# The recurrence of a macaron layer as 86 chunks of 24 tokens in place of 228 chunks of 9

## The reference, cut to what matters

```python
B_all = einsum('bsd,nd->bsn', xn, B_w) + B_b
states = A_pow * cumsum(B_all / max(A_pow, 1e-8))          # a linear scan over the tokens
ssm_out = einsum('bsn,dn->bsd', states, C_w) + C_b
def step(h, xt):                                           # 4096 tokens, one after the other
    cat = concatenate([xt, h])                             # 1024 + 512
    ff1 = tanh(cat @ ff1_w.T + ff1_b)
    ff2 = tanh(cat @ ff2_w.T + ff2_b)
    t_i = sigmoid((cat @ ta_w.T + ta_b) * 0.1 + (cat @ tb_w.T + tb_b))
    return ff1 * (1 - t_i) + t_i * ff2
out = x + h_all @ out_w.T + out_b
```

## Time and profile before

| | us |
|---|---|
| median of 3 runs | 1722.78 |
| lowest and highest of them | 1721.22, 1829.82 |
| the profiled execution | 1719.35 |
| its span on the slowest core | 1717.8 |
| spans of the 8 cores | 1714.5 to 1717.8 |
| first matmul of the recurrence | 874.89 |
| first matmul of the projection behind it | 1084.68 |

### The profile page before, as it was taken

One profiled execution on the slowest core, in us unless ns is written; L12 is line 12 of the kernel. 1 busy time (PEld: TensorE's weight loads), 2 busy tenths in 40 slices (PEclk: granted clock), 3 DMA queues, 4 the chain that ended last, 5 costly groups with the idle time before them and its releaser, 6 DMA issues. The chain is left out here.

```text
span 1717.8 us, 29950 instructions; the slowest of 8 cores (1714.5 to 1717.8 us)
## 1 busy us (share of the span) xinstructions
PE 1279.5 (74%) x9089; PEld 860.0 (50%) x9107; DVE 1172.6 (68%) x2126; ACT 958.1 (56%) x1428; POOL 642.6 (37%) x668
## 2 busy tenths in 40 slices
PE   0000087698898998998659987357699999998999
PEld 0000065465565665654348866135465655655644
DVE  4898568687687776774266666458776776777741
ACT  0426167766776766674246654146666666665651
POOL 0000322555756746547500024221633535334332
PEclk9999999899999999999869999579999999998999
DMA  9590210212122221114120000111111111200111
GB/s 290 176 334 4 62 38 13 62 37 51 38 50 62 62 51 38 51 38 118 55 50 2 2 1 2 52 59 50 50 50 64 61 50 56 81 26 26 50 38 62
DMA packets 35765, 105.66 MB, mean 62 GB/s; under 512 B 4756, under 2 KB 14100, under 8 KB 34584
## 3 DMA queue, kind: packets, MB, share of 16 engines
q1 hardware_dynamic: 24568, 95.08, 16.7%
q0 software_dynamic: 11040, 8.66, 3.5%
HBM read 84.58 MB, written 25.70 MB: 64 GB/s over the span
## 5 line engine op out<-in xcount | busy, mean ns | idle before, releaser
L587 PE MATMUL bank<-xqT,w1q 128*128 128x258 bf16 (+1 forms) x4352 | 575.4, 277 | 111.2 <-DVE y L891 110.6
L587 PEld LDWEIGHTS bank<-xqT,w1q 128*128 128x128 fp8e4 x4352 | 417.4, 100 | 277.4 <-issue 149.3
L608 PE MATMUL bank<-w2q,q 128*128 128x512 fp8e4 x2112 | 535.2, 383 | 0.0
L921 DVE SCALAR_TENSOR_TENSOR y<-bank,convws,y 128x256 f32<-128x256 f32 (+1 forms) x544 | 256.4, 471 | 270.3 <-ACT y L738 269.2
L1055 POOL TENSOR_TENSOR y<-y,Rb 128x1024 f32<-128x1024 f32 (+1 forms) x136 | 322.8, 2403 | 179.3 <-ACT Rb L763 179.3
L738 ACT ACTIVATE y<-bank,convbs,convws 128x256 f32<-128x256 f32 (+1 forms) x544 | 293.1, 551 | 165.0 <-PE bank L587 161.3
L608 PEld LDWEIGHTS bank<-w2q,q 128*128 128x128 f16 x2112 | 206.1, 98 | 166.1 <-issue 7.9
L891 DVE SCALAR_TENSOR_TENSOR y<-bank,convws,y 128x256 f32<-128x256 f32 (+1 forms) x544 | 253.8, 467 | 0.1
L689 ACT ACTIVATE y<-y 128x1024 f32<-128x1024 f32 (+1 forms) x136 | 139.9, 1029 | 149.5 <-DVE y L891 149.3
L832 DVE TENSOR_TENSOR M<-M,ab 128x1024 f32<-128x1024 f32 (+1 forms) x119 | 199.4, 1676 | 2.2 <-ACT ab L701 2.2
L711 ACT ACTIVATE q<-y,qoff 128x1024 f16<-128x1024 f32 (+1 forms) x136 | 151.8, 1117 | 65.8 <-POOL y L1055 62.3
(11 more groups left out here) (159 smaller groups left out, 1328.7 us busy)
## 6 DMA issues: line engine op xcount, KB each, us to landing
raw<-w1T SPq DMA_DIRECT2D x8, 2048.0 KB, 35.2
raw<-w2T SPq DMA_DIRECT2D x8, 2048.0 KB, 17.8
xg<-xall SPq DMA_DIRECT2D x18, 512.0 KB, 5.2
x1t<-xall SPq DMA_DIRECT2D x17, 512.0 KB, 4.1
basebuf<-x1t SPq DMA_DIRECT2D x17, 512.0 KB, 3.1
xg<-basebuf SPq DMA_DIRECT2D x16, 512.0 KB, 4.6
x2buf<-xg SPq DMA_DIRECT2D x16, 512.0 KB, 2.9
x1t<-x2buf SPq DMA_DIRECT2D x16, 512.0 KB, 4.3
```

The source lines that it names most:

```text
L587: mm = pe.matmul(pA[n % 4][:, 0:tw + 2], w1q[:, c, k * P:(k + 1) * P], xqT[j % 3][:, c, 0:tw + 2], start=c == 0, stop=c == DC - 1)
L608: pe.matmul(pB[e % 2][:], q[:, qs, kh, :], w2q[:, kh, 512 * h:512 * h + 512], start=kh == 0, stop=False)
L921: dve.scalar_tensor_tensor(v, pA[n % 4][:, 0:tw], convws[:, 3 * k:3 * k + 1], v, ALU.mult, ALU.add).then_inc(conv1_done, 1)
```

## The change

The chunks become longer and fewer: 86 chunks of 24 tokens, so 17 + 24 = 41 steps of 86 columns. The gate blocks of a step are no longer taken one by one. They lie in four banks of PSUM, and consecutive steps use the two halves of the eight banks in turn. For each half of the hidden units one bank holds ff1 and ff2 (four blocks, 344 columns) and one holds the time gate (two blocks, 172 columns). ScalarE takes a bank with one tanh, so 4 in a step, and VectorE makes half of the hidden units with one `mixd`, `mixu`, `hcur` of 172 columns, so 6 in a step.

A bias column can't serve a bank with several blocks, so the biases are added by TensorE: one matmul for each block with the transposed biases `bT` (44 rows: the values in bf16 in rows 0 to 11, what the rounding left in rows 32 to 43) and `pick`, which is 1 in the rows of that block. That makes 72 matmuls of 86 columns in a step: 12 for biases, 12 of `Wp`, 48 of `Wh`. `b44`, `pick` and `bT` are made ahead of the recurrence, on VectorE with one transpose on TensorE. The four `Wh` parts are taken in two groups, parts 0 and 1 when the first half of `hcur` is there, parts 2 and 3 when the second is. And `bias_dve` is moved from behind the last step to between steps 0 and 1.

```diff
-CN = 228
-CL = 9
+CN = 86
+CL = 24
 CW = 17
-SJC = 230
+SJC = CN + 1
...
-    gate = [[at(f'gate{i}{j}', GB + (3 * j + i) * 928, [P, CN]) for j in range(2)] for i in range(3)]
-    mixd = [at(f'mixd{j}', GB + 5568 + j * 928, [P, CN]) for j in range(2)]
-    mixu = [at(f'mixu{j}', GB + 5568 + 1856 + j * 928, [P, CN]) for j in range(2)]
-    assert GB + 5568 + 3712 <= YB + YR * T * 4
-    hcur = [at(f'hcur{j}', MB + j * 1824, [P, KC, CN], BF16) for j in range(2)]
+    st_ = at('states', YB + 16384 + 8704, [P, WLEN + 16])
+    sJ = at('sJ', YB + 16384 + 8704 + 8768, [P, CL, SJC], BF16)
+    GB = YB + 16384 + 8704 + 8768 + 4192
+    gateF = [at(f'gateF{i}', GB + i * 1376, [P, 2, 2, CN]) for i in range(2)]
+    gateT = [at(f'gateT{i}', GB + 2752 + i * 704, [P, 2, CN]) for i in range(2)]
+    mixd = [at(f'mixd{i}', GB + 4160 + i * 704, [P, 2, CN]) for i in range(2)]
+    mixu = [at(f'mixu{i}', GB + 5568 + i * 704, [P, 2, CN]) for i in range(2)]
+    pick = at('pick', GB + 6976, [P, 12, CN], BF16)
+    b44 = at('b44', GB + 9056, [P, 44])
+    bT = at('bT', GB + 9248, [P, P], BF16)
...
+    def ssm_pe():
+        pe.wait_ge(bias_in, 4)
+        pe.wait_ge(bsb_done, 17)
+        pe.transpose(pM[0:44, 0:P], b44[:], idf[:]).then_inc(bias_mm, 1)
...
+        dve.wait_ge(round_done, 8 * NT1)
+        dve.scalar_tensor_tensor(bcr[:, 8:12], bcr[:, 8:12], 0.1, bcr[:, 12:16], ALU.mult, ALU.add).then_inc(bias_in, 1)
+        dve.memset(b44[:], 0.0).then_inc(bias_in, 1)
+        dve.wait_ge(bias_in, 2)
+        dve.tensor_copy(b44[:, 0:12], bcr[:, 0:12]).then_inc(bias_in, 1)
+        dve.tensor_copy(b44[:, 32:44], bcr[:, 0:12]).then_inc(bias_in, 1)
+        dve.tensor_tensor(pick[0:44], idb[0:44, 0:12].unsqueeze(2).to_broadcast([44, 12, CN]),
+                          idb[0:44, 32:44].unsqueeze(2).to_broadcast([44, 12, CN]), ALU.add)
...
-        dve.scalar_tensor_tensor(bcr[:, 8:12], bcr[:, 8:12], 0.1, bcr[:, 12:16], ALU.mult, ALU.add).then_inc(ssm, 1)
-        dve.wait_ge(ssm, 7)
-        dve.tensor_scalar(bcr[:, 8:12], bcr[:, 8:12], 0.5, None, ALU.mult)
+        dve.wait_ge(ssm, 6)
         dve.tensor_copy(carry[:], st_[:, 2047:2048])
         dve.tensor_scalar(tofs[:], tofs[:], 2048.0, None, ALU.add)
-        dve.tensor_copy(sJ[:], st_[:, 108:108 + CL * SJC].rearrange('p (c k) -> p k c', k=CL))
+        dve.tensor_copy(sJ[:], st_[:, 126 - CL:126 - CL + CL * SJC].rearrange('p (c k) -> p k c', k=CL))
+        dve.wait_ge(bias_mm, 1)
+        dve.tensor_copy(bT[0:44, :], pM[0:44, 0:P]).then_inc(ssm, 1)
+        dve.wait_ge(ssm, 7)
+        dve.tensor_tensor(bT[32:44, :], pM[32:44, 0:P], bT[32:44, :], ALU.subtract)
...
-            pool.wait_ge(h_done, 4 * s + 4)
+            pool.wait_ge(h_done, 2 * s + 2)
             pool.tensor_copy(hv[:, :, :, s - CW], hcur[s % 2][:]).then_inc(hc_done, 1)
...
+    def slots(half, kind):
+        if kind == 0:
+            return [(2 * f + c, 512 * f + P * (2 * half + c), 4 * f + 2 * half + c) for f in range(2) for c in range(2)]
+        return [(c, 1024 + P * (2 * half + c), 8 + 2 * half + c) for c in range(2)]
     def cfc_pe():
+        parts = [(half, kind) for half in range(2) for kind in range(2)]
         for s in range(NSTEP):
             u = s - CW
-            s_in = sJ[:, u % CL, u // CL + 2:u // CL + 2 + CN]
+            s_in = sJ[:, u % CL, u // CL + 1:u // CL + 1 + CN]
             h_in = hcur[(s + 1) % 2]
-            def cols(i):
-                c0 = 512 * (i % 3) + P * (i // 3)
-                return slice(c0, c0 + P)
-            for i in range(6):
-                n = 12 * s + i
-                if n >= 8:
-                    pe.wait_ge(gate_done, n - 7)
-                mm = pe.matmul(bank[n % 8][:, 0:CN], Wp[:, cols(i)], s_in, start=True, stop=s == 0)
+            gb = bank[4 * (s % 2):4 * (s % 2) + 4]
+            for i, (half, kind) in enumerate(parts):
+                if s >= 2:
+                    pe.wait_ge(gate_done, 4 * (s - 2) + i + 1)
+                for at_, c0, r in slots(half, kind):
+                    o = gb[i][:, CN * at_:CN * at_ + CN]
+                    pe.matmul(o, bT[0:44, :], pick[0:44, r, :], start=at_ == 0, stop=False, skip_group_check=True)
+                    mm = pe.matmul(o, Wp[:, c0:c0 + P], s_in, start=False, stop=s == 0, skip_group_check=True)
                 if s == 0:
                     mm.then_inc(gate_mm, 1)
             if s:
-                for kk in range(KC):
-                    pe.wait_ge(h_done, 4 * (s - 1) + kk + 1)
-                    for i in range(6):
-                        n = 12 * s + i
-                        mm = pe.matmul(bank[n % 8][:, 0:CN], Wh[:, kk, cols(i)], h_in[:, kk, :], start=False, stop=kk == KC - 1)
-                        if kk == KC - 1:
-                            mm.then_inc(gate_mm, 1)
-            for i in range(6, 12):
-                n = 12 * s + i
-                if n >= 8:
-                    pe.wait_ge(gate_done, n - 7)
-                mm = pe.matmul(bank[n % 8][:, 0:CN], Wp[:, cols(i)], s_in, start=True, stop=s == 0)
-                if s:
-                    for kk in range(KC):
-                        mm = pe.matmul(bank[n % 8][:, 0:CN], Wh[:, kk, cols(i)], h_in[:, kk, :], start=False, stop=kk == KC - 1)
-                mm.then_inc(gate_mm, 1)
+                pe.wait_ge(h_done, 2 * (s - 1) + 1)
+                for i, (half, kind) in enumerate(parts):
+                    for at_, c0, r in slots(half, kind):
+                        o = gb[i][:, CN * at_:CN * at_ + CN]
+                        for kk in range(2):
+                            pe.matmul(o, Wh[:, kk, c0:c0 + P], h_in[:, kk, :], start=False, stop=False, skip_group_check=True)
+                pe.wait_ge(h_done, 2 * (s - 1) + 2)
+                for i, (half, kind) in enumerate(parts):
+                    for at_, c0, r in slots(half, kind):
+                        o = gb[i][:, CN * at_:CN * at_ + CN]
+                        for kk in range(2, 4):
+                            mm = pe.matmul(o, Wh[:, kk, c0:c0 + P], h_in[:, kk, :], start=False, stop=kk == 3, skip_group_check=True)
+                    mm.then_inc(gate_mm, 1)
     def cfc_act():
         for s in range(NSTEP):
-            for i in range(12):
-                n = 12 * s + i
-                b, f = i // 3, i % 3
-                act.wait_ge(gate_mm, n + 1)
-                if n >= 6:
-                    act.wait_ge(h_done, (n - 6) // 3 + 1)
-                act.activation(gate[f][b % 2][:], bank[n % 8][:, 0:CN], AF.Tanh, bias=bcr[:, 4 * f + b:4 * f + b + 1],
-                               scale=0.5 if f == 2 else 1.0).then_inc(gate_done, 1)
+            gb = bank[4 * (s % 2):4 * (s % 2) + 4]
+            for half in range(2):
+                if s:
+                    act.wait_ge(h_done, 2 * (s - 1) + half + 1)
+                act.wait_ge(gate_mm, 4 * s + 2 * half + 1)
+                act.activation(gateF[half][:].rearrange('p f b c -> p (f b c)'), gb[2 * half][:, 0:4 * CN], AF.Tanh).then_inc(gate_done, 1)
+                act.wait_ge(gate_mm, 4 * s + 2 * half + 2)
+                act.activation(gateT[half][:].rearrange('p b c -> p (b c)'), gb[2 * half + 1][:, 0:2 * CN], AF.Tanh,
+                               scale=0.5).then_inc(gate_done, 1)
     def cfc_dve():
         for s in range(NSTEP):
-            for b in range(4):
-                n = 4 * s + b
-                f1, f2, tt = gate[0][b % 2], gate[1][b % 2], gate[2][b % 2]
-                hh = hcur[s % 2][:, b, :]
-                dve.wait_ge(gate_done, 3 * n + 2)
-                dve.tensor_tensor(mixd[b % 2][:], f2[:], f1[:], ALU.subtract).then_inc(mix_d, 1)
-                dve.wait_ge(gate_done, 3 * n + 3)
+            if s == 1:
+                bias_dve()
+            for half in range(2):
+                n = 2 * s + half
+                f1, f2, tt = gateF[half][:, 0], gateF[half][:, 1], gateT[half][:]
+                hh = hcur[s % 2][:, 2 * half:2 * half + 2, :]
+                dve.wait_ge(gate_done, 4 * s + 2 * half + 1)
+                dve.tensor_tensor(mixd[half][:], f2, f1, ALU.subtract).then_inc(mix_d, 1)
+                dve.wait_ge(gate_done, 4 * s + 2 * half + 2)
                 dve.wait_ge(mix_d, n + 1)
-                dve.scalar_tensor_tensor(mixu[b % 2][:], tt[:], 1.0, mixd[b % 2][:], ALU.add, ALU.mult).then_inc(mix_u, 1)
+                dve.scalar_tensor_tensor(mixu[half][:], tt, 1.0, mixd[half][:], ALU.add, ALU.mult).then_inc(mix_u, 1)
                 dve.wait_ge(mix_u, n + 1)
                 if s >= CW + 2:
                     dve.wait_ge(hc_done, s - CW - 1)
-                if s in (CW - CL, CW):
-                    c = 1 if s == CW - CL else 0
-                    dve.scalar_tensor_tensor(hh, mixu[b % 2][:], 0.5, f1[:], ALU.mult, ALU.add).then_inc(mix_h, 1)
-                    dve.wait_ge(mix_h, b + 1 + (4 if s == CW else 0))
-                    dve.tensor_tensor(hh[:, c:c + 1], hh[:, c:c + 1], pcs[:, 4:5], ALU.mult).then_inc(h_done, 1)
```

(31 more changed lines are left out.)

## The result

The changed kernel takes 1793.2 us (median of 5 runs) against 1721.2 for the kernel before: a ratio of 1.042, with a 95% interval of 1.041 to 1.043. It is slower by 4.2%, where I had forecast 1689 and a range of 1679 to 1715. The profiled execution has a span of 1791.6 us on its slowest core (core 2).

What follows compares the result with a forecast made beforehand. TensorE's 60 matmuls and their chain bound warm-up steps; GpSimd's copy adds 2.2 us to late ones. Recurrence 26.9 plus projection 5.8 saves 32.7 us: 1686.7 profiled, 1690.1 median, 1689 taken; range 1679 to 1715.

Steps and rivals of the forecast that it cites:

- A step after the change, TensorE's share: Recurrence step: 72 matmuls of 86 columns at 0.038 us each, 2.7 us, where 60 matmuls took 6.31.
- The sign that was named: Recurrence: a matmul spacing above 0.047 us would make the forecast wrong upward, as would a late `mixd` over 0.5.
- half clock: Recurrence: TensorE, working 2.7 of 3.8 us, stays at half clock; 5.5 us a step, 1751 us; chance 0.04.
- The rival that ended slower: Recurrence: short matmul pairs have a TensorE floor of 0.078 us or more; at 0.095, 1803 us; chance 0.08.
- The chain: Recurrence step: 0.75 us from `hcur` to first tanh, then 3.01 through VectorE's six operations; 3.76 us a step.
- ScalarE's slope: Tanhs in the recurrence: ScalarE costs 0.84 ns a column, so 0.55 us for 344 columns and 0.41 for 172.
- The last 24 steps: End of the recurrence: 4.0 us a step, with GpSimd copying 344 columns in place of 912.
- The copy's block on `mixd`: Last 24 steps: GpSimd's copy blocks VectorE until 1.44 us after `hcur`, `mixd` wants 1.41; 0.1 a step counted.
- the rival of a block until the copy's end: Last 24 steps: the copy holds `mixd` until it ends, 0.5 us a step, 12 more, 1701 us; chance 0.10.
- The projection: Behind the last `hcur`: copy and release to first matmul take some 2.4 us in place of 8.16, 5.8 less.
- The wait for `obr`: Step 1: VectorE waits for the moved bias row's DMA, landing up to 12.7 us after issue; some 10 us lost.
- The start: Ahead of the recurrence: making `pick` and `bT` delays GpSimd by 1.0 us and adds 0.6, together 1.6 us.

Runs made afterwards that it cites:

- with 128 rows: Changed kernel with the bias matmuls padded with zeros from 44 to all 128 rows, nothing else edited; 1676.5 us, 0.975 of before.
- without bias matmuls: Changed kernel with the bias matmuls left out of the loop, so the gates have no biases; 1677.1 us, 0.975 of before.
- both kernels with 24 changes a step: The changed kernel (44-row bias matmuls), 1793.2 us, and its padded version with 64 rows in the bias matmuls, 1792.1 us.
- the chunks alone: Kernel before with only the new sizes, 86 chunks of 24 tokens, and nothing else of the change; 1719.5 us, 0.999 of before.

## Why the prediction was wrong

**The step that failed is "A step after the change, TensorE's share".** It gave all 72 matmuls of a step a spacing of 0.038, taken from runs of matmuls of one shape, and said of the 44-row ones only that no row shows them. The bounds, 0.025 and 0.095, came from matmuls and weight loads with 128 rows too, so they could not hold what lay outside: 0.143 for each of the 24 alternating matmuls. The bias matmuls were then costed at nothing by the slack of 0.2 us that this spacing left. The runs put 24 x 0.104 = 2.5 us a step on the alternation. No rival was made of a change of row count between neighbours. The sign that was named, a spacing above 0.047, did come.

**The clock.** The rival "half clock" came true in part, and its reason did not: it made the clock depend on TensorE's idle share. In the changed kernel the records show no idle time and the clock is 0.71; with 128 rows TensorE is idle for 5.8 of 40 us, without bias matmuls for 10.9, and the clock is 1.00. What is shown is that the clock fell in both kernels with 24 changes a step (0.71 and 0.74) and was at 0.99 or more from 905 to 1035 in every variant of the changed kernel with 8 or fewer. But the alternation is not needed for it: the chunks alone, where all matmuls have 128 rows, have 0.88 from 905 to 1075, with falls to 0.50 (from 1002 to 1004, for one), and TensorE is recorded busy there for 79% of the time, less than with 128 rows in the changed kernel and more than without bias matmuls. Why the clock falls is open, also because the records can't show what TensorE does between the starts. Its price, 48 `Wh` matmuls 0.072 apart and not 0.039, is 1.6 us a step. Together with the 2.5 that makes 4.1, of which the slack of about a microsecond takes part; measured are 3.0 (6.80 against 3.79). That the clock alone would be worth 1.6 is worked out, not shown by a run of its own.

**The rival that ended slower** set a floor for every short pair, with 0.078 as the point of decision. The mean over the step is indeed 6.80 / 72 = 0.094, so its side and its price were right (0.095 gave 1803). That was luck: 0.095 was the recorded length of a weight load, and 0.094 is a mean of 24 matmuls 0.143 apart and 48 that are 0.072 apart. Its mechanism was wrong, since the same pairs with 128 rows come 0.039 apart. The Trainium skill's rule (TensorE: Matmul & The Clock Gate, "Back-to-back issue gap"), 81 ns for 128 columns, is not borne out: 55 ns at 128 columns, and 39 at 86 over whole steps.

**What held, as the kernels without the alternation show.** The spacing: 0.039 for 0.038. The chain: 3.63 us a step for 3.76; most of the difference is the tanh of 344 columns, 0.46 for 0.55. ScalarE's slope was right: without a bias column 172 columns take 319 ns and 344 take 460, 0.82 ns a column, and with one 86 take 336 (the chunks alone) and 228 take 453, again 0.82. What I overlooked is that the tanh with a bias column is some 0.09 us longer at equal width, and the change takes that column away. The last 24 steps: 3.79 for 4.0. The copy's block on `mixd` is gone: with 128 rows `mixd` runs from 1040.42 in its usual 0.34 us, inside a copy recorded from 1039.28 to 1041.04. So the rival of a block until the copy's end falls, and the 8 us that a lock for the whole instruction would have cost did not come. The projection: 2.25 behind the last `hcur` (its three terms add up to 2.26, not to the 2.4 that I wrote). The wait for `obr`, in the changed kernel: VectorE waits 5 us and step 1 starts 14.5 behind the DMA's issue (874.54 to 889.04), 16.1 were computed; placing the row later brought 5 us of the some 10 that were charged at the start, as the row's own 3.5 us stay in the recurrence. The start: from the last `BATCH_NORM_AGGREGATE` of the first FFN to the first `mixd` the changed kernel takes 37.6 us (839.38 to 876.98) and the kernel before 35.8 (841.74 to 877.52), the same on all eight cores. That is 1.8 later where 1.6 was charged, though by other parts: GpSimd's second small operation took 3.39, and the `sJ` cast 2.71 in place of 3.82. With 128 rows the same stretch takes 35.7, GpSimd's operation 1.24, and nothing is lost. Summed up against the kernel with 128 rows, the profiled time is 10 us under the 1686.7 computed: 8.5 in the recurrence (162.0 from first `mixd` to last `hcur` for 170.5) and 1.7 at the start. The median lay no higher than the profiled execution, where 3.4 had been added, so the forecast of 1689 is 12.5 over.
